# Decoder layer on one core: early queries' tiles with 32 keys, values of four heads a block, later keys as a product of their own

## The reference

```python
x = layernorm(x + linear_attention_block(x))        # phi = elu + 1, then a table-GELU feed-forward
x = layernorm(x + cross_attention(x, ctx, mask))
x = layernorm(x + shared_and_expert_ffn(x))         # top 2 of 7 gates, one expert matrix
```

```python
scores = einsum('bhqd,bhkd->bhqk', q, k) / sqrt(8)
m = mask[:, None, :, None] + future[None, None, :, :]   # mask is over QUERIES, future is k > q
scores = where(m != 0, -1e9, scores)
attn = softmax(scores, axis=-1)
ctx = einsum('bhqk,bhkd->bqhd', attn, v) @ WO
```

## Time and profile before

| | |
|---|---|
| median of 3 runs | 604.05 us (602.84 to 606.14) |
| the profiled execution | 608.8 us, span 607.1 us |
| TensorE busy | 533.2 us, 88% of the span (mean granted clock 0.969) |
| VectorE busy | 417.6 us, 69% |
| ScalarE busy | 371.0 us, 61% |
| GpSimd busy | 340.5 us, 56% |
| first k_exp transfer of phase 3 | 251.5 us |
| last store done | about 607 us |

### The profile page before, as it was taken

How to read it: one execution, slowest core, us unless ns; L and a number is a source line. 1 busy time by engine, 2 the same in 40 slices (tenths; PEclk the granted TensorE clock), 3 DMA queues, 4 the chain that set the end, 5 groups by cost and what they waited for, 6 DMA issues and landing times.

```text
span 607.1 us, 23038 instructions
## 1 busy us (share of the span) xinstructions
PE 533.2 (88%) x9312; PEld 371.9 (61%) x9312; DVE 417.6 (69%) x1453; ACT 371.0 (61%) x643; POOL 340.5 (56%) x619
## 2 busy tenths in 40 slices
PE   2799999989999999888999999998989989999741
PEld 1477676756777777635666666666656656666530
DVE  2577777756677766345677797777876887779743
ACT  2365665647777777646666666676666756766521
POOL 6766666656755554531345546754575457544564
PEclk9899999999999999969999999999999999999876
DMA  6600000000000000011111111111111111101001
GB/s 170 181 32 2 3 1 3 3 2 1 1 2 1 2 1 2 9 25 29 32 31 29 42 30 49 39 35 28 49 49 25 27 49 48 28 25 32 20 19 35
DMA packets 24987, 17.97 MB, mean 30 GB/s; under 512 B 3121, under 2 KB 21425, under 8 KB 24881
## 3 DMA queue, kind: packets, MB, share of 16 engines
q1 hardware_dynamic: 24448, 16.43, 10.3%
q10 hardware_dynamic: 432, 0.07, 0.1%
HBM read 9.67 MB, written 4.19 MB: 23 GB/s over the span
## 4 chain that ended last, share of the span: by engine, by line
PE 61%; SPq 11%; issue 7%; POOL 6%; ACT 5%; DMA 5%; DVE 4%; POOLq 0%; DVEq 0%; ACTq 0%
SPq L391 11%; PE pair L1143 7%; PE pair L1127 7%; PE pair L1158 6%; PE pair L1177 6%; PE pair L1210 6%; PE pair L1018 5%; DMA k_exp<-k_sb 4%; PE pair L1096 4%; PE pair L1187 4%; PE pair L1109 3%; PE pair L1196 3%; PE pair L1089 3%; ACT gel L684 3%; PE pair L1165 2%
## 5 line engine op out<-in xcount | busy, mean ns | idle before, releaser
L684 ACT ACTIVATE gel<-pair 128x1024 f32<-128x1024 f32 x64 | 65.6, 1025 | 76.8 <-PE pair L1177 76.8
L908 DVE TENSOR_REDUCE neg_max<-pair 128x16 f32<-128x1024 f32 x64 | 60.9, 952 | 24.5 <-PE pair L1165 24.4
L1158 PE MATMUL pair<-k_exp,qT 64*32 64x256 f32 (+1 forms) x1024 | 58.1, 505 | 13.1 <-DMA k_exp<-k_sb 10.0
L1143 PEld LDWEIGHTS pair<-w,gel 128*128 128x128 f32 x512 | 60.7, 192 | 9.0 <-issue 7.2
L1187 PEld LDWEIGHTS pair<-v,gel 128*32 128x32 f32 x4096 | 41.5, 110 | 36.2 <-ACT gel L684 31.2
L1143 PE MATMUL pair<-w,gel 128*128 128x128 f32 x512 | 62.1, 275 | 1.0 <-ACT gel L650 1.0
L1187 PE MATMUL pair<-v,gel 128*32 128x18 f32 x4096 | 48.0, 187 | 14.1 <-ACT gel L684 11.3
L1127 PE MATMUL pair<-hT,w 128*128 128x512 f32 x128 | 58.5, 597 | 2.0 <-ACT lev L645 1.3
L678 ACT ACTIVATE gel<-gel,row_scale 128x512 f32<-128x512 f32 x80 | 54.4, 720 | 6.3 <-DVE gel L921 6.2
L300 POOL TENSOR_SCALAR veps_c<-mv_c 128x4 f32<-128x4 f32 x16 | 3.7, 230 | 95.4 <-issue 89.0
L1177 PE MATMUL pair<-ident,gel 128*128 128x128 f32 x384 | 52.5, 280 | 0.4 <-ACT gel L678 0.4
(11 more groups left out here) (126 smaller groups left out, 1236.7 us busy)
## 6 DMA issues: line engine op xcount, KB each, us to landing
X<-in_x SPq DMA_DIRECT2D x16, 256.0 KB, 3.0
cT<-in_ctx SPq DMA_DIRECT2D x16, 256.0 KB, 2.9
out_rows<-X SPq DMA_DIRECT2D x16, 256.0 KB, 2.6
k_exp<-k_sb SPq DMA_DIRECT2D x160, 16.0 KB
w<-in_L_attn_w SPq DMA_DIRECT2D x2, 256.0 KB, 3.5
w_kv<-in_L_attn_wk SPq DMA_DIRECT2D x1, 64.0 KB, 3.2
w_q<-in_L_attn_wq ACTq DMA_DIRECT2D x1, 64.0 KB, 3.0
w_kv<-in_L_attn_wv SPq DMA_DIRECT2D x1, 64.0 KB, 3.1
```

The source lines that it names most:

```text
L684: nc.scalar.activation(pT[par], pair[par][:, :, :].rearrange("p a c -> p (a c)"), ACT.Copy).then_inc(pT_ready, 1)
L908: nc.vector.tensor_reduce(neg_max[par][:, :].rearrange("p (a h) -> p a h", a=2), scores, AX.X, ALU.max, negate=True).then_inc(max_ready, 1)
L1143: last = nc.tensor.matmul(bank(6 + q)[:, P * t:P * (t + 1)], gel[:, q, f, P * t:P * (t + 1)], w_2[:, f, :], start=(f == 0), stop=(f == NF ...
L1158: nc.tensor.matmul(pair[t % 2][b * QW:(b + 1) * QW, half, 0:HH * width], qT[p][rows, batch + first:batch + first + QW], keys, start=True, ...
```

## The change

- Odd tiles keep 32 keys a head to the end: 16 heads of 32 keys are 512 columns, four heads a block of 128. `turn_probabilities` transposes 4 blocks in place of 8, `copy_pT` copies 512 columns, `probability_rows` for odd tiles are 512 wide.
- The values get a second form v4 with four heads a block. GpSimd's new `spread_v(g)` copies it from v2 in four copies of 256 columns on 32 partitions, between the norm rows ln_b and ln_c of the step, and waits for v2_ready. `weigh_values` of odd tiles has 16 products of 36 columns.
- The later keys of masked queries become four products of 144 columns with the matrix `future` (128 keys rows by queries: 1 where the key is a late one and the query masked). It is made by VectorE once a group: the new `future_keys(g, q)` stands in slot 2 of step g-1, ahead of that slot's `shift`, and waits for `mask_loaded`. Its input is a row of the mask spread over all partitions, loaded by SyncE: `load_mask(s+1)` in step s >= 0, behind `spread_k(s+1)` and `load_ctx(s+2)` and ahead of `store(s-2)`; group 0's is loaded at the start. The host lays out one more array, mask_early.
- GpSimd's `future_keys`, its two calls a step and `row_masked` go.
- Causal products cover the newest 32 keys of each head alone: 256 columns for even tiles too.
- GpSimd's constants at the start grow by the zeroing and the ones columns of both v4 buffers and by late_key. The causal constant is built in y2's memory, and the two odd probability buffers lie in the memory of gel.

```diff
-        row_masked = sb("row_masked", [P, NT])
+        late_key = sb("late_key", [P, 1])
+        mask_rows = [sb(f"mask_rows{i}", [P, 2, P], I32) for i in range(2)]
+        future = [sb(f"future{i}", [P, 2, P]) for i in range(2)]
-        causal = sb("causal", [P, HH, S])
...
-        s_early = [big[:, 1024:2048], sb("s_early1", [P, H * S])[:, :]]
-        pT = [big[:, 2048 + 1024 * i:2048 + 1024 * (i + 1)] for i in range(2)]
+        s_early = [big[:, 1024 + 512 * i:1024 + 512 * (i + 1)] for i in range(2)]
+        pT = [big[:, 2048:3072], big[:, 3072:3584]]
...
+        v4 = [sb(f"v4{i}", [P, 2 * TG, QB, QB, HV]) for i in range(2)]
+        causal = y2[:, :, :].rearrange("p t d -> p (t d)").rearrange("p (h k) -> p h k", k=S)
...
+            def load_mask(g, p):
+                src = mask_early[2 * g:2 * g + 2, :].rearrange("n p -> (n p)")
+                sp.dma_start(mask_rows[p][:, :, :].rearrange("p n q -> p (n q)"),
+                             src.partition_broadcast(P)).then_inc(mask_loaded[p], 16)
+
...
                 if exists(s + 2):
                     after(sp, xv_done, s + 1)
                     load_ctx(s + 2, p)
+                if exists(s + 1) and s >= 0:
+                    after(sp, future_ready, s)
+                    load_mask(s + 1, 1 - p)
                 if exists(s - 2):
                     store(s - 2)
...
+                const(nc.gpsimd.memset(late_key[b * S + QW:(b + 1) * S, :], 1.0))
...
                 const(nc.gpsimd.memset(v2[i][:, :, :, :, :], 0.0))
                 for h in range(2):
                     const(nc.gpsimd.memset(v2[i][h * S:(h + 1) * S, :, :, h, DH:HV], 1.0))
+                const(nc.gpsimd.memset(v4[i][:, :, :, :, :], 0.0))
+                for j in range(QB):
+                    const(nc.gpsimd.memset(v4[i][j * QW:(j + 1) * QW, :, :, j, DH:HV], 1.0))
                 const(nc.gpsimd.memset(moe_out[i][:, :, 2 * D + NE:], LOWEST))
             pool.sem_inc(const_ready)
...
                 nc.gpsimd.memset(buffer[:, 0:HDMA, :], 0.0).then_inc(zeroed, 1)
-            def future_keys(m):
-
-                if m < 2:
-                    pool.wait_ge(const_dve, 5)
-                    pool.wait_ge(down_done, NG)
-                else:
-                    pool.wait_ge(p_xposed, 2 * m - 2)
-                rows = s_early[m % 2].rearrange("p (h k) -> p h k", k=S)[:, :, QW:]
-                nc.gpsimd.tensor_copy(rows, row_masked[:, 2 * m + 1:2 * m + 2].unsqueeze(2)
-                                      .broadcast_to([P, H, S - QW])).then_inc(future_ready, 1)
+            def spread_v(g, q):
+
+                pool.wait_ge(v2_ready, g + 1)
+                apart(pool)
+                heads = v2[q].rearrange("p u (i j) h e -> p u i j h e", j=2)
+                for j in range(2):
+                    for h in range(2):
+                        slot = 2 * j + h
+                        nc.gpsimd.tensor_copy(
+                            v4[q][slot * QW:(slot + 1) * QW, :, :, slot, 0:DH],
+                            heads[h * S:h * S + QW, :, :, j, h, 0:DH]).then_inc(v4_ready, 1)
+                        pool.wait_ge(v4_ready, g * QB + slot + 1)
             def phase3(s, p):
-                if exists(s):
-                    future_keys(2 * s + 1)
                 if exists(s + 2) and not early(s):
                     copy_y(s + 2, p)
                 g, q = s + 1, 1 - p
...
                     after(pool, y2_xposed, r)
                     ln_rows_pool(pool, ln_b, r, lambda t: X[:, r * TG + t, :],
                                  lambda t: y2[:, t, :], mv_b, negm_b, rstd_b[0])
+                if exists(g):
+                    spread_v(g, q)
                 if exists(s - 2):
                     o = s - 2
                     ln_deviation(pool, ln_c, o, mv_c, veps_c, rstd_c)
                     ln_rows_pool(pool, ln_c, o, lambda t: moe_out[p][:, t, 0:D],
                                  lambda t: X[:, o * TG + t, :], mv_c, negm_c, rstd_c)
-                if exists(s + 1) and not early(s):
-                    future_keys(2 * s + 2)
             pipeline(pool, phase1, last=NG)
             phase2(0, 0)
...
                 for half in range(1 if n % 2 else 2):
                     act.wait_ge(sub_ready, shifted(n, half))
-                    rows = probability_rows(n).rearrange("p (h k) -> p h k", k=S)
-                    part = rows[:, :, 0:QW] if n % 2 else rows[:, HH * half:HH * (half + 1), :]
+                    rows = probability_rows(n)
+                    part = rows if n % 2 else rows[:, GW * half:GW * (half + 1)]
                     nc.scalar.activation(part, part, ACT.Exp, scale=row_scale[:, n:n + 1])\
                         .then_inc(exp_ready, 1)
             def copy_pT(n, par):
                 act.wait_ge(p_xposed, n + 1)
                 after(act, pv_done, n - 1)
-                nc.scalar.activation(pT[par], pair[par][:, :, :].rearrange("p a c -> p (a c)"),
-                                     ACT.Copy).then_inc(pT_ready, 1)
+                flat = pair[par][:, :, :].rearrange("p a c -> p (a c)")
+                nc.scalar.activation(pT[par], flat[:, 0:GW] if n % 2 else flat, ACT.Copy)\
+                    .then_inc(pT_ready, 1)
             def collect(n, t, p):
...
                 after(dve, p_xposed, n - 3 if n % 2 else n - 1)
-                rows = probability_rows(n).rearrange("p (h k) -> p h k", k=S)
+                rows = probability_rows(n).rearrange("p (h k) -> p h k", k=width)
                 if n % 2:
-                        rows.rearrange("p (a h) k -> p a h k", a=2)[:, :, :, 0:QW], scores,
+                        rows.rearrange("p (a h) k -> p a h k", a=2), scores,
...
                 ln_statistics(dve, ln_c, g, lambda t: moe_out[p][:, t, 0:D], stats_c, mv_c,
                               ln_c.offs, g)
+            def future_keys(g, q):
+
+                dve.wait_ge(mask_loaded[q], g // 2 * 16 + 16)
+                after(dve, pv_done, g * TG - TG)
+                nc.vector.tensor_scalar(future[q][:, :, :], mask_rows[q][:, :, :], 0.0,
+                                        late_key[:, 0:1], ALU.not_equal, ALU.mult)\
+                    .then_inc(future_ready, 1)
+
             def phase3(s, p, slots=range(TG)):
                 prev, old, q = s - 1, s - 2, 1 - p
                 for t in slots:
+                    if t == 2 and exists(s + 1):
+                        future_keys(s + 1, q)
                     if exists(s) if t < TG - 1 else exists(s + 1):
                         shift(s * TG + t + 1, (t + 1) % 2)
                     if t == 1 and exists(prev):
...
                                          start=True, stop=False)
                 for half in range(2):
                     rows = slice(half * FH, half * FH + QW)
-                    future = causal_bf[rows, :].rearrange("p (h k) -> p h k", k=S)[:, :, S - width:]
+                    newer = causal_bf[rows, :].rearrange("p (h k) -> p h k", k=S)[:, :, QW:]
                     for b in range(QB):
-                        last = nc.tensor.matmul(pair[t % 2][b * QW:(b + 1) * QW, half, 0:HH * width],
-                                                ident_bf[rows, rows], future,
-                                                start=False, stop=True)
+                        row = pair[t % 2][b * QW:(b + 1) * QW, half, 0:HH * width]
+                        last = nc.tensor.matmul(
+                            row.rearrange("p (h k) -> p h k", k=width)[:, :, width - QW:],
+                            ident_bf[rows, rows], newer, start=False, stop=True)
                 last.then_inc(s_done, 1)
             def turn_probabilities(n, t):
                 flat = pair[t % 2][:, :, :].rearrange("p a c -> p (a c)")
-                for i in range(HH):
+                for i in range(HH // 2 if n % 2 else HH):
                     if i % (HH // 2) == 0:
                         pe.wait_ge(exp_ready, shifted(n, 2 * i // HH))
-                    if i == 0 and n % 2:
-                        pe.wait_ge(future_ready, n // 2 + 1)
                     last = nc.tensor.transpose(flat[:, P * i:P * (i + 1)],
                                                probability_rows(n)[:, P * i:P * (i + 1)], ident[:, :])
                 last.then_inc(p_xposed, 1)
...
                 pe.wait_ge(pT_ready, n + 1)
                 after(pe, xatt_ready, n)
+                if n % 2:
+                    pe.wait_ge(v4_ready, (n // TG + 1) * QB)
+                    pe.wait_ge(future_ready, n // TG + 1)
+                    for b in range(QB):
+                        nc.tensor.matmul(
+                            bank(7)[b * QW:(b + 1) * QW, 0:H * HV],
+                            future[p][:, t // 2, b * QW:(b + 1) * QW],
+                            v2[p][:, t // 2 * QB + b, :, :, :].rearrange("p i h e -> p (i h e)"),
+                            start=True, stop=False)
+                    for i in range(QB):
+                        for b in range(QB):
```

(10 more changed lines are left out.)

24 lines of the change are left out of this document (12 added, 12 removed).

## The result

The changed kernel took **673.28 us** (median of 4 runs, 672.75 to 676.86); the kernel before, run beside it on the same chip, took 605.1. The ratio is **1.1126** (95% interval 1.1043 to 1.1209): slower by 11%. The profiled execution took 673.23, its span is 671.3 against the 607.1 of before. The prediction had 660 with a range of 642 to 684: the sign holds, the measured time lies in the range, and 13 us are missing from the sum.

The account below looks back on a forecast made before the run. Bounds: TensorE's own work and a nearly equal ring through SyncE. 38.4 + 3.9 + 6.7 - 1.4 + 4.4 + 4 = +56 us: 665 on the profiled execution, 660 for the median; range 642 to 684, forecast by itself 643 to 673.

Parts of the forecast that it names:

- The ring: Attention steps: store, k_exp, scores, VectorE, GpSimd, next store; with the mask wait 23.37 us a step in place of 19.88.
- The clock: Attention steps: TensorE's clock falls after idling for the mask wait; 0.3 us a step added, +4 in all.
- +2.4: Step 0, without a store: tile 3 ends at 285.9 against 283.5, 2.4 us later.
- +3.8: Step 1, without a store: tile 3 ends at 304.6 against 300.8, 3.8 us later.
- +6.7: Steps 0 to 2 together: the first store comes 6.7 us late.
- Rival (a): Clock falls in every step, low past k_sb: some 2 us more in twelve steps, 684 us; chance 0.20.
- Constants: Kernel start: GpSimd's added memsets delay TensorE, which hardly regains it later; +4.4 us.
- spread_v: hidden: GpSimd, attention steps: four copies, 1.8 us, covered by idle time ahead of the last normalisation; costed at nothing.
- rival (d): GpSimd: spread_v's copies outgrow their cover, over 1.2 us each; 1 us a step more, 673 us; chance 0.04.
- The 1.7: TensorE, attention steps: smaller turning, pT copy, values and future products save 1.7 us a step, 27 over 16 groups.
- -1.4: Tail: the last odd tile's transposes and its copy shrink, saving 1.4 us.
- Rival (c): TensorE's queue sets the step and its 1.7 us come off each: faster, 581 us; chance 0.03.

Follow-up runs that it names:

- the two ways of taking the wait away: Changed kernel with VectorE's future operation moved to slot 3, 609.04 us; changed kernel with the mask rows loaded one group further ahead, 607.38 us.
- the kernel with the filler: Changed kernel plus six unread products of 256 columns in TensorE's gap ahead of turning tile 3; 670.77 us.
- With the ring cut: Changed kernel with mask load one group further ahead and store one step later, 594.13 us; kernel before with only the later store, 599.0 us.
- the future operation is out of the way of the shift: Changed kernel with earlier mask load, later store, v4 constants in the feed-forward gap and future operation in slot 3; 586.06 us.

## Why the prediction was right, point by point

**The ring and its new member: right, and shown.** The step was put together from the issue of the mask load (7.71), its landing (3.0), 0.40 for the operation and resuming, and 12.26 from the shift of tile 3 to the store. Measured over the eleven steps: store to issue 7.99; issue to the start of the future operation 3.33 against 3.05; from there to the next store 12.57 against 12.61. The operation, bounded by 0.19 and 0.62 and taken as 0.35, measured 0.351. The kernel before with nothing but the wait lost as much as the change, and the two ways of taking the wait away gave all but 3 to 4 us of it back: the attribution does not rest on the sum.

**Two terms of the step were a little small, and for a reason in the sum.** "Some k_exp blocks are longer ... I leave that out" left out a real 0.28: blocks of 7.1 to 7.4 in place of 6.66 come in four of eleven steps, and one cT issue took 1.24 instead of 0.44. The kernel before has such blocks too, 7.0 to 7.7 in three of its eleven steps, which run from 19.23 to 21.00, and its 19.88 is the mean over them. So the prediction set a new step without delays against an old mean with them. The changed kernel's two quickest steps, from 343.01 and from 485.11, take 23.25 and 23.32, 0.1 under what was put together. The landing was taken as 3.0 and is 3.2 in the median:

```profile
DMA to landing us min/median/max: 3.0/3.2/4.4
```

Together +0.5 a step: 23.89 against 23.37, 5.7 us over eleven steps. By the rule of the Trainium skill (DMA: Bandwidth & Descriptors, Anatomy of one DMA) it would have been 2.3, an estimate; the page gives the rule for DMAs that GpSimd issues, this load is issued by SyncE, and the trace does not agree, its shortest is 3.0.

**The clock: put in the wrong steps.** The prediction added 0.3 a step. The clock did fall after each gap, as the Trainium skill (TensorE: Matmul & The Clock Gate, HAM oscillation) describes and as the windows show, but in the steps with a store the stretch from the future operation on is no longer than with the clock held at 0.96: that term is zero, and that it stood in the sum helped the total by luck. Steps 0 to 2 were the term that failed: "+2.4", "+3.8", "+6.7" to the first store, against 12.6 measured. No store holds SyncE there; TensorE is on the chain, and the same fall of the clock is paid in full. The chain of waits of the changed kernel in step 1 (start us, us, what):

```profile
302.43 4.14 DMA mask_rows<-in_mask_early
...
308.31 0.73 ACT gel L695
309.04 0.04 issue
309.08 1.11 PE pair L1202 x4
310.20 0.85 PE pair L1044 x4
311.05 0.64 PE pair L1214 x8
311.69 0.48 PE pair L1221 x32
312.17 2.35 PE pair L1253 x6
```

Behind exp it stays on TensorE up to the next k_exp issues. Windows of the same kernel, inside step 0 and inside step 1:

```profile
288.00:294.00 6.00, 5.57 (x78) 4.13 (x79) 2.70 (x6) 2.55 (x5) 2.17 (x5) 0.56 0.01 3
306.00:312.00 6.00, 2.92 (x48) 2.50 (x48) 4.52 (x8) 3.39 (x6) 1.45 (x4) 0.58 0.00 2
```

A clock of 0.56 to 0.58 is the level of 1.2 GHz for most of the window. The five groups of the chain, from 309.08 to the scores at 314.52, take 5.44; at full clock, in a step of the kernel with the filler, they take 4.00 (405.67 to 409.67), a wait for the copy included. From the shift of tile 3 to the next k_exp issue the prediction allowed 8.1 in step 0 and 10.1 in step 1; the rows have 10.75 and 12.1, together 4.6 more. From the issue of the mask load to the shift of tile 3 the three steps take 3.66, 4.43 and 4.30 where 3.4 was allowed, another 2.2. Against that, k_exp in step 0 was issued 0.7 quicker than assumed and step 0 began 0.2 sooner; that leaves the 5.9 that are missing. The 4.6 can be followed in rows at the two levels of the clock: in step 1 the 1.44 above; in step 0, from the scores behind tile 3 to the next projection, 3.89 (289.55 to 293.44) where the kernel before takes 2.19 (283.42 to 285.61), 1.7 more; the rest lies in turning, transposes and products of tile 3 at the low clock. But no run took the low clock away in those steps, so that it is the clock is read from rows and not shown by an experiment. Rival (a) had such a price, 2 us a step, in twelve steps; it came in two.

**Constants: right.** GpSimd's first deviation starts at 25.23 in place of 20.88, +4.35 where 4.4 were predicted. At the first k_exp issue the two profiled executions are 3.5 apart, but the kernels without v4 differ there by 2 among themselves, and over all runs the constants cost about 5, as above.

**spread_v: hidden, right.** Its row in GpSimd's timeline:

```profile
452.22 1.83 POOL L542 COPY v<-v 32x256 f32<-32x256 f32 x4 [4.14 <-ACT v L759]
457.52 0.23 POOL L304 TENSOR_SCALAR veps_c<-mv_c 128x4 f32<-128x4 f32 x1 [3.47 <-DVE mv_c L296]
```

Four copies in 1.83, behind which GpSimd still idles 3.47. They take 0.41 each; rival (d) needed 1.2.

**TensorE's saving: right that it is worth next to nothing between stores, wrong in two parts.** The 1.7 were 1.3 of work and a pT copy that TensorE waits for, 0.43. The work measured 1.2: turning saved 0.44 a tile start to start (0.93 before, 0.49 after), and 0.1 of an even tile's causal product. But the values gave nothing, "0.05" a tile being within the rows: 463.75 to 464.43 is 0.68, where a tile's 32 products took about 0.67. "-1.4" in the tail did not come either: thirteenth store to end, 42.65 against 42.5. From the turning of the last odd tile to the output product the rows are 0.76 quicker (638.58 to 645.06, before 573.76 to 581.00), but that turning starts 0.76 later behind the store. Rival (c), a gain of 27 us from TensorE, priced the saving at 1.7 a step. With the ring cut 0.7 of it comes off the step, and 1.0 once the future operation is out of the way of the shift (19.30 to 18.34). As the change stands, its condition (the mask there when VectorE asks) failed in each of 15 steps.

**The sum.** Predicted +56 on the profiled execution, measured +64: +5.7 from the steps, +5.9 from steps 0 to 2, +1.5 from the tail, -4 for the clock term that was in the wrong place and -0.9 at the start make +8.2. The other 5 of the 13 us that the median is off: the profiled execution of the kernel before lay 0.8% over its median, and the prediction took that off again, while the changed kernel's, 673.23, is its median. With all this the measured 673.28 stands at the very end of the 643 to 673 that the forecast had by itself; the stated range had room above only because it reached up to rival (a). The mechanism was right and the size was low: every error but the clock term and the start pointed the same way.

## What to carry to other kernels

When a load is added to a queue that a ring runs through, find the moment at which its consumer asks and the moment at which it is issued; if the consumer asks first, the full landing time goes on the step, however small the transfer, and a load one step earlier takes it off again; here it cost nothing, since the two buffers of the mask rows were enough. An in-order queue that holds a store in front of the next step's loads makes a ring of the whole kernel, and work taken off the busiest engine then buys next to nothing in those steps until that ring is cut. A stall that also lets the clock fall cost nothing more in the steps where the filler raised the clock again; where TensorE was on the chain the rows say that it cost some 2 us a step.

## What the runs showed of the hardware that was not expected

- The same issue on SyncE is not always as short: 0.43 in most of the sixteen mask loads, but 0.76, 1.29 and 1.50 in three; ten k_exp issues 6.66, at times 7.0 to 8.9 over all runs. On a ring such delays add up, some 0.3 a step.
- A load of 128 KB that spreads one row over all partitions lands in 3.2 (3.0 to 4.4), no faster than the cT load of twice its bytes, 2.9. The cT load in front of it is not the reason: issued ahead of cT it still took 3.3 (3.0 to 4.2), and cT, then behind it, 3.6. Whether it is the spreading over partitions was not tried.
- Half as many products of twice the columns take more than half the time: 16 products of 36 columns (32 records) take 0.41 start to start (464.02 to 464.43), 32 of 18 columns (64 records) 0.67.
- GpSimd's copy of 256 columns on 32 partitions takes 0.41, that of 512 on 128 partitions 0.62, so a quarter of the partitions and half of the columns save a third.
